# Graph layer on one core: weight and key sums finished inside the query stage, graph products first in the mix, experts combined by accumulating transfers

## The reference, cut to what matters

```
xn  = layernorm(x)
gnn = xn @ W.T + bias                                   # W: scatter of edge_weight
q,k,v = split(xn @ W_qkv); q,k = relu(rmsnorm(q)), relu(rmsnorm(k))
kv  = einsum('bhnd,bhne->bhde', k, v)
out = einsum('bhnd,bhde->bhne', q, kv) / (q . k.sum + eps)
x   = x + gnn + out @ W_out + b_out
t   = rmsnorm(layernorm(x)) * norm_scale
top 2 of t @ gate_w + gate_b, probabilities p
y   = sum over the 2 experts: p * (swiglu(t @ w1 + b1) @ w2 + b2)
return x + layernorm(x) + y
```

## Time and profile before

| What | us |
|---|---|
| median of 3 runs | 1178.75 (1176.22 to 1180.52) |
| profiled execution, its own time | 1176.67 |
| its span | 1174.9 |
| PE busy | 956.7 (81%) |
| DVE busy | 785.2 (67%) |
| ACT busy | 271.7 (23%) |
| POOL busy | 166.1 (14%) |
| share of PE in the chain that ended last | 44% |
| share of "issue" in it | 15% |

### The profile page before, as it was taken

The page is one execution under the profiler, slowest core; times in us unless marked ns, Lnnn a source line. Parts: engine busy times, 40 slices in busy tenths (PEclk is TensorE's granted clock), DMA queues, the critical chain, the costliest instruction groups (busy, mean ns, idle before and its releaser), DMA issues.

```text
span 1174.9 us, 18153 instructions
## 1 busy us (share of the span) xinstructions
PE 956.7 (81%) x5569; PEld 594.8 (51%) x5570; DVE 785.2 (67%) x1245; ACT 271.7 (23%) x455; POOL 166.1 (14%) x186
## 2 busy tenths in 40 slices
PE   3428999999999789973698999999728999999940
PEld 2324666666666446541366666566514555555510
DVE  4888788888888698447576666763463555555555
ACT  0652222222222344460011111110002222122100
POOL 1232000000000100000223322221102111111432
PEclk9657999999999989995699989998858999999985
DMA  7545333333333445558913333335318999762759
GB/s 229 177 137 193 123 142 143 143 143 143 142 143 139 179 162 180 187 209 235 299 61 138 122 106 106 106 106 204 127 33 293 309 349 343 274 241 110 210 168 304
DMA packets 86474, 210.27 MB, mean 179 GB/s; under 512 B 29395, under 2 KB 38553, under 8 KB 81321
## 3 DMA queue, kind: packets, MB, share of 16 engines
q1 hardware_dynamic: 70345, 171.27, 42.4%
q0 software_dynamic: 12208, 24.42, 6.9%
q10 hardware_dynamic: 3888, 14.16, 3.0%
HBM read 128.37 MB, written 81.42 MB: 179 GB/s over the span
## 4 chain that ended last, share of the span: by engine, by line
PE 44%; DVE 20%; issue 15%; DMA 8%; SPq 4%; ACT 4%; POOL 2%; DVEq 1%; POOLq 0%; ACTq 0%
PE windows L882 11%; PE bank L721 9%; PE bank L900 6%; PE bank L777 6%; PE bank L822 4%; DMA arena<-in_w_flat 3%; DMA arena<-y_dram,arena 2%; DVE arena L1347 2%; DVE arena L1254 2%; PE bank L873 2%; POOL arena L611 1%; SPq L443 1%; PE windows L740 1%; DVE arena L1247 1%; DVE arena L1260 1%
## 5 line engine op out<-in xcount | busy, mean ns | idle before, releaser
L822 PE MATMUL bank<-arena 128*125 128x512 f16 x960 | 220.7, 389 | 2.7 <-POOL arena L594 2.7
L721 PE MATMUL bank<-arena 128*125 128x512 f16 x960 | 217.5, 384 | 0.0
L822 PEld LDWEIGHTS bank<-arena 128*125 (+1 forms) x960 | 133.8, 140 | 78.5 <-issue 7.2
L721 PEld LDWEIGHTS bank<-arena 128*125 (+1 forms) x960 | 129.6, 138 | 73.2 <-issue 3.8
L882 PE MATMUL windows<-arena 128*128 x648 | 149.7, 381 | 0.0
L777 PE MATMUL bank<-arena 128*128 128x416 f16 (+1 forms) x576 | 103.7, 340 | 0.0
L882 PEld LDWEIGHTS windows<-arena 128*128 128x128 f16 x648 | 63.8, 98 | 65.7 <-issue 1.6
L1254 DVE SCALAR_TENSOR_TENSOR arena<-arena 128x2048 f16<-128x2048 f32 x32 | 73.0, 2285 | 12.7 <-ACT arena L972 12.7
L777 PEld LDWEIGHTS bank<-arena 128*128 128x128 f16 x576 | 55.7, 97 | 44.5 <-issue 0.6
L900 PE MATMUL bank<-arena 128*128 x324 | 74.3, 379 | 1.7 <-DVE arena L1527 1.7
L1247 DVE TENSOR_TENSOR arena<-windows,arena 128x1024 f32 x49 | 59.8, 1220 | 16.1 <-issue 8.2
(11 more groups left out here) (223 smaller groups left out, 1285.6 us busy)
## 6 DMA issues: line engine op xcount, KB each, us to landing
arena<-in_w_flat SPq DMA_DIRECT2D x32, 1024.0 KB, 6.5
split_dram<-arena SPq DMA_DIRECT2D x64, 512.0 KB, 3.8
arena<-split_dram SPq DMA_DIRECT2D x48, 512.0 KB
y_dram<-arena SPq DMA_DIRECT2D x9, 1536.0 KB, 6.5
y_dram<-arena ACTq DMA_DIRECT2D x27, 512.0 KB
arena<-in_x SPq DMA_DIRECT2D x20, 448.0 KB
arena<-in_w_qkv SPq DMA_DIRECT2D x8, 1024.0 KB, 6.2
arena<-split_dram SPq DMA_DIRECT2D x32, 256.0 KB, 6.3
```

The lines of the kernel that those rows point to most:

```text
L721: mm = pe.matmul(bank[b][0:TT, :], xt[:, l, k, tok(i)], wkv[:, r, k, c0:c0 + 512], start=(k == 0 and n == 0), stop=(k == KT - 1 and n == 2))
L822: mm = pe.matmul(bank[half][0:TT, :], a_[:, l, k, tok(i)], w_[:, r, k, c0:c0 + 512], start=(m == 0 and k == 0 and c == 0), stop=(m == 1 an ...
```

## The change

Four things move.

1. `w_acc` is split in turn 1 of the query stage instead of behind the stage; SP writes it to DRAM at the end of turn 1, between the requests for pieces 27 and 28, and reads it back (`wg`) at the end of turn 2, ahead of the requests for pieces 30 and 31. The split of the key-value sums (`kv_split`, 6 larger instructions instead of 16 small ones) moves into unit 2 of turn 0. Pieces 22 and 23 are split by DVE after units 0 and 1 instead of before unit 0. The first block of query weights is loaded before the key stage ends, into a buffer of its own. To make room, `make` uses no `key_hot` tile: it multiplies in place, with a second wait.
2. In the mix, `xt` by `wg` comes first. For tiles 0 and 1 these products lie between the first eight attention units. In `mix_tile` both halves' graph products run before the wait for `at_done`, and units 6 and 7 of a group move into the tile that needs them.
3. `base` is stored straight into the output. Each block's rows are scaled by their probability on ACT (`scale_y`) and added to the output by an indirect transfer that accumulates (`add_block`), one after the other. `y_dram`, its zeroing, the gathers and the combination at the end are gone. Routing gets 40 small matmuls for the probability of each slot.
4. The output has 128 spare rows for empty slots.

```diff
-            sp.wait_ge(kv_mm, 4 * NT)
-            for h in range(2):
-                load_wq(0, h)
 ...
+            load_wq(0, 0)
+            sp.wait_ge(kv_mm, 4 * NT)
+            load_wq(0, 1)
+            next_pieces(-1)
+            for t in range(2):
+                next_pieces(t)
+                next_wq(t)
             for k in range(KT):
                 sp.wait_ge(acc_lo, k + 1)
...
+            next_pieces(2)
+            next_wq(2)
             sp.wait_ge(acc_out, 16 * 2 * KT)
...
+            next_pieces(3)
```

```diff
-                v.tensor_tensor(pairs_of(key_hot), columns, cols(key16), ALU.is_equal).then_inc(hot_key, 1)
-                v.wait_ge(hot_key, n + 1)
-                v.tensor_tensor(pairs_of(one_hot[s][:, 1, :]), pairs_of(key_hot), cols(whi), ALU.mult)
-                v.tensor_tensor(pairs_of(one_hot[s][:, 2, :]), pairs_of(key_hot), cols(wlo), ALU.mult).then_inc(hot_ready, 1)
+                key_hot = pairs_of(one_hot[s][:, 1, :])
+                v.tensor_tensor(key_hot, columns, cols(key16), ALU.is_equal).then_inc(hot_key, 1)
+                v.wait_ge(hot_key, 2 * n + 1)
+                v.tensor_tensor(pairs_of(one_hot[s][:, 2, :]), key_hot, cols(wlo), ALU.mult).then_inc(hot_key, 1)
+                v.wait_ge(hot_key, 2 * n + 2)
+                v.tensor_tensor(key_hot, key_hot, cols(whi), ALU.mult).then_inc(hot_ready, 1)
```

```diff
+            def q_turn(t, groups=0, first=False, split=False, last=False):
...
+                    if first and u < 2:
+                        piece_lo(NT + 1, u)
+                    if first and u == 2:
+                        kv_split()
...
+                    if split and u >= 3:
+                        for k in range(3 * u - 9, min(3 * u - 6, KT)):
+                            acc_part_lo(k)
```

```diff
             def mix_tile(i, h, t, attend=True):
+                for half in range(2):
+                    pe.wait_ge(x1_half, 2 * i - 1 + half)
+                    if h == 0:
+                        attend_unit(6 + half, t, PAIRS * t + 6 + half)
+                    elif attend:
+                        attend_unit(2 + half, t + 1, PAIRS * (t + 1) + 2 + half)
+                    mix_part(i, bank[0:2], 0, half, 0, KT)
                 if h == 0:
                     pe.wait_ge(at_done, START + PAIRS * (t + 1))
                 for half in range(2):
...
+                    mix_part(i, bank[0:2], 1, half, 0, KT)
```

```diff
+            def add_block(b, s):
+                pool.tensor_copy(to_idx[s], to_of[:, bass.ds(b, 1)]).then_inc(to_ready, 1)
+                pool.wait_ge(to_ready, b + 1)
+                pool.wait_ge(y_scaled, b + 1)
+                if not (isinstance(b, int) and b == 0):
+                    pool.wait_ge(y_added, 16 * b)
+                apart(pool)
+                pool.indirect_dma_start(out=out, out_offset=bass.IndirectOffsetOnAxis(ap=to_idx[s], axis=0), in_=ysb[s], in_offset=None,
+                                        compute_op=ALU.add).then_inc(y_added, 16)
```

More of the change, by code:

```diff
@@ L597, in _ @@
                 attend_lo(j, 0, j)
+            for j in range(2):
+                attend_lo(j, 1, PAIRS + j)
             pool.wait_ge(mixc_in, 80)
@@ L785, in _ @@
                 q_units(t)
-            pe.wait_ge(q_split, START + 6 * KT)
-            pe.wait_ge(q_evac, START + 3 * KT)
-            pe.wait_ge(kvb_ready, 1)
-            for g in range(3):
-                pe.matmul(bank[g][:, 0:GRP[g][1]], ones, qss[:, g, 0:GRP[g][1]], start=True, stop=True).then_inc(eps_mm, 1)
             def attend_unit(j, g, unit):
@@ L799, in attend_unit, with mix_part @@
                 mm.then_inc(at_mm, 1)
+            def mix_part(i, o, m, half, a, b):
+                a_, w_ = ((xt, wg), (ut, wo))[m]
+                c0 = half * 512
+                for k in range(a, b):
+                    for c, (l, r) in enumerate(((0, 0), (0, 1), (1, 0))):
+                        mm = pe.matmul(o[half][0:TT, :], a_[:, l, k, tok(i)], w_[:, r, k, c0:c0 + 512],
+                                       start=(m == 0 and k == 0 and c == 0), stop=(m == 1 and k == KT - 1 and c == 2))
+                if m == 1 and b == KT:
+                    mm.then_inc(mix_mm, 1)
@@ L800, in _ @@
+            pe.wait_ge(acc_done, START + GROUPS)
+            pe.wait_ge(wg_in[0], 32)
+            mix_part(0, bank[6:8], 0, 0, 0, 4)
+            pe.wait_ge(q_split, START + 6 * KT)
+            pe.wait_ge(q_evac, START + 3 * KT)
+            for g in range(3):
+                pe.matmul(bank[g][:, 0:GRP[g][1]], ones, qss[:, g, 0:GRP[g][1]], start=True, stop=True).then_inc(eps_mm, 1)
+            mix_part(0, bank[6:8], 0, 0, 4, 8)
             pe.wait_ge(eps_ready, 3)
+            pe.wait_ge(wg_in[1], 32)
@@ L867, in _ @@
             mm.then_inc(token_mm, 1)
+            pe.wait_ge(probs_ready, 1)
+            for u in range(2 * NT):
+                for c in range(2):
+                    mm = pe.matmul(bank[1][:, 0:BLOCKS], place_hot[0:TT, u, :], block_p[0:TT, c, u, :], start=(u == 0 and c == 0), stop=(u == 2 * NT - 1 and c == 1))
+            mm.then_inc(prob_mm, 1)
             def row_T(b, s, q):
@@ L1069, in mix_period @@
                     mix_sqrt(i, h)
-                if not first:
-                    tt_copy(i - 1)
+                tt_copy(i - 1)
                 if not last:
```

411 lines of the change are left out of this document (204 added, 207 removed).

## The result

The changed kernel takes 1212.3 us (median of 4 runs, 1211.8 to 1215.75) against 1179.6 for the kernel before: a ratio of 1.029, 95% interval 1.025 to 1.032. It is slower by 33 us, where the prediction said 18 to 19.

What follows compares the result with a forecast made beforehand. PE is at work almost everywhere, idle at four kinds of place. 2.3 + 10.3 + 18.4 + 8.4 - 32.6 + 46.6 - 0.7 - 33 = +19.7; on 1176.67 that is 1196.4, so 1198 us; range 1155 to 1235.

Steps and rivals of the forecast that it cites:

- the experts: Expert blocks: scaling fits ACT's idle time and an add takes 7.4 a block, below the pitch of 8.87: cost 0.
- the end: Behind the last evacuation: the combination goes, only scaling and the last adds at 6 each remain: -33.
- The key stage: `make` in the key stage: one extra 0.23 wait per tile in PE's chain, ten tiles: +2.3.
- Turns 0 and 1: Start of the query stage: pieces requested later and `kv_split` on DVE make PE wait: +10.3, bounds -5 and +12.
- Turn 2: Query stage: piece 28's request stands behind sixteen graph transfers on SP, so ACT and PE wait: +18.4, bounds 12 and 22.
- Turn 3: Query stage: pieces 30 and 31 come late behind query weights and `wg` loads on SP: +8.4, bounds 0 and 14.
- Query end to tile 1: From query stage to end of tile 1: earlier splits and graph products remove the 21.89 wait: -32.6, bounds -40 and -25.
- Tiles 2 to 9: Mix: PE waits 13.3 four times for units 6 and 7, behind `mix_in` on POOL: +46.6, bounds 0 and +60.
- the accumulate becomes the bound: Rival for the expert blocks: chained adds set the pace from 7.5 a transfer, giving 1223 or 1293; chance 0.13.

Runs made afterwards that it cites:

- the edit alone: Kernel before, with only the in-place columns of `make` and their second wait added: 1181.1 us, ratio 1.0020.
- the later run: Changed kernel with only `kv_split` moved from turn 0 to turn 2: 1207.7 us, ratio 1.0256.
- the three orders tried later: Changed kernel with SP's pieces ahead of graph stores and weight loads (1195.5), graph stores issued by POOL (1192.8), or SP reordered transfer by transfer (1195.7).
- the POOL edit: Changed kernel with only `mix_in` of the odd tile put behind units 6 and 7 on POOL: 1184.2 us, ratio 1.0062.
- the units edit: Changed kernel with all eight attention units again computed a group ahead, graph products still first: 1168.0 us, ratio 0.990.
- the plain write: Changed kernel with scaled rows overwriting the output instead of being accumulated, same transfers, waits and order: 1202.4 us, ratio 1.0208.
- the earlier gathers: Changed kernel with each gather of expert rows issued one block earlier on POOL: 1207.9 us, ratio 1.0239.
- the last run: Changed kernel with SP reordered transfer by transfer, `kv_split` later, pieces 22 and 23 first, units a group ahead, gathers earlier, POOL's final add wait removed: 1126.3 us.
- the run with SP's order worked out: Changed kernel with SP's pieces, query weights, graph stores and graph weights reordered transfer by transfer, pieces 30 and 31 taken at units 1 and 3: 1195.7 us.

## Why the prediction came out as it did

It was right in sign and within its range; the sum, 19.7, was 15 short of the 35.2 between the two profiles. Seven of its nine terms are within 4 of what was measured, and their misses, three of them too high, cancel. The 15 are the other two: the experts, 9.4, and the end, 5.8. By its steps:

- *The key stage* was mis-sized: two of a tile's columns lie in PE's chain, not one (18 waits instead of 9), so +5 instead of 2.3, above the bound of 4.6. Shown by the edit alone, which gave +6.1 in that stage.
- *Turns 0 and 1*: right in size, 11 against 10.3, and in mechanism. Less the 5.2 of the key stage, PE's two large waits end at 432.9 and 444.1, where the prediction had 434.1 and 445.1; `kv_split` with the key sums took DVE 6.4, against 6.2. The first wait stays when `kv_split` is moved and goes with the pieces, the second goes with `kv_split`, as in the prediction's chain; it was the expectation of the later run that had it otherwise. Moved away, the two are worth 4.6 and 6.2.
- *Turn 2*: the mechanism as described, the ACT wait at the place named; 15 against 18.4, as SP was held for 16.13 and not 18.01, and PE stood for 13.77 and not 16.4.
- *Turn 3*: 11 against 8.4. The term was the bytes ahead of piece 30, 6.5 MB at about 350 GB/s; ACT had the piece 23.0 after the turn's start and not 19.5. The rate was as taken, 339 GB/s from 528 to 552 with the engines busy 0.96, but 8.1 MB moved in that time. In the three orders tried later, 7 to 10 us of turns 2 and 3 remain.
- *Query end to tile 1*: -30.9 against -32.6, with the wait of 6.46 for the fifth unit where 7 was forecast.
- *Tiles 2 to 9*: +42.7 against +46.6; waits of 15.35 and then 12.1 to 13.1 against 13.3. The chain named (x, `mix_in`, units 6 and 7) is the one that the POOL edit cuts, for 28.2, and the units edit for 44.3.
- *The experts* failed as a step: "cost 0" rested on 7.4 a block being below 8.87. The average is below, but POOL is in order, and `gather` for a later block stands behind the wait for the add ahead of it. Late gathers then meet the expert weights. The prediction weighed the adds as a chain of their own and did not ask what is queued behind them. Its rival "the accumulate becomes the bound" was nearer in place, but not in mechanism: the pitch stayed at 8.87 and the loss is in single blocks. Shown by the plain write (experts 248.1) and by the earlier gathers (251.1).
- *The end*: -27.2 against -33. The adds of blocks 25 and 26 took 6.1 and 5.8, as the 6 that was taken; what was missed is the 5.1 behind the last landing, for POOL's drain. The prediction's own terms, 1136 and 1.3 and 6, make 1143.3 and not 1142, so -32 rather than -33. The drain is shown in part by the last run. That an add lands in 6 was a guess between 2.62 and 8.40, and the median of 6.2 is luck; in the experts single adds took up to 10.5.

On the transfer itself, the plain write landed in 3.4 and the accumulate in 6.2, in the median. For one transfer of 512 KB the Trainium skill (DMA: Bandwidth & Descriptors, "Anatomy of one DMA") gives 2.0 plus the bytes over 436 GB/s, by estimate 3.2: the trace agrees for the write, and not for the accumulate.

Open: how much of the 7 to 10 us left in turns 2 and 3 would go if piece 28 were requested in the idle stretch ahead of it, and how much of the rest comes from the 256-byte runs of the graph stores and how much from the bytes alone.

## What to carry to other kernels

When a step moves, list what stands behind each of its instructions on every in-order queue, issuing queues included: the sixteen stores, the wait for x and the wait for the last add each cost what was queued behind them, not what they took themselves. A queue of its own takes a transfer out of that line, but not off the transfer engines: look at how busy these are in the stretch, and in the one ahead of it. A cover (graph products ahead of the wait) is worth only what it covers: compare when the awaited thing is produced now, not when it was before. And a step below the pitch in the mean can still cost where it shares an engine with the step that feeds the next block.

## What the runs showed of the hardware

An accumulating scatter of 128 rows of 4 KB landed in 6.2 us in the median against 3.4 for the same scatter as a write; POOL was held 1.6 against 1.0; beside expert weights four adds in a row took 7.7 to 11.8 (the run with earlier gathers). POOL's drain at the program's end took 4.5 us when it began behind the last landing, and every other engine passed the program's last semaphore only behind it, at 1210.0 where it ended at 1209.9; begun before the landing it ended 2.2 behind it. In the kernel before it ended 2.0 behind POOL's last landing as well, and 2.9 ahead of the end of the program, which SP's stores set, so that it cost nothing. In the run with SP's order worked out, with sixteen 256 KB stores in 256-byte runs in the stretch from 490 to 535, the transfer engines were busy 0.90 to 1.02 of the time at 250 to 352 GB/s. Two loads of 256 KB landed 14.1 and 19.4 after their issue when POOL's queue carried these stores beside them, and 3.3 and 4.4 when SP issued the stores behind them.
